# A causal attention block with top-2 expert layer: scores and row maxima of two heads in the two halves of the array's rows, the mask added by VectorE, and maxima three blocks ahead

## The chip, the cores and the metric

One core of a Trainium2 chip runs the whole program. The metric is the device time of one execution in microseconds; three executions of the kernel before gave 769.35, 771.28 and 776.9 us, median 771.28.

## What is computed

The input is x of 8 sequences x 512 rows x 128 columns, fp32. Attention has 16 heads of 8 dimensions with rotary embedding, a causal mask and softmax. Its result is added to x and layer-normalized. Then every row goes through a shared expert and through the two best of 8 routed experts (hidden width 256), and is layer-normalized again.

```python
q = rope(x @ Wq); k = rope(x @ Wk); v = x @ Wv      # 16 heads of 8
attn = softmax(where(causal, q @ k.T / 8 ** 0.5, -inf))
x = layernorm(x + (attn @ v) @ Wo)
rw, sel = top_k(x @ router_w.T + bias, 2); rw = softmax(rw)
ffn = lambda w1, w3, w2: (silu(x @ w1) * (x @ w3)) @ w2
x = layernorm(x + ffn(shared) + sum over r of rw[r] * ffn(expert sel[r]))
```

## The kernel before, in words

**Order of the work.** Nothing is scheduled at run time. The program lays events on a clock of its own, whose unit is one score unit (a full PSUM bank of 512 score columns, 40 to a sequence, 320 in all). The table `AT` gives each kind of event its place on that clock and `LATER` shifts a kind on one engine; each engine issues its events in that order (`line`), and semaphores do the rest. So an engine's instructions stand in a fixed row, and one that waits holds up all behind it.

**Attention.** q and k are projected with two fp32 matmuls each (L652), turned by VectorE (L877), summed and split into three bf16 parts that add up to the fp32 value (L315, L319, L323, with ScalarE's L542 and L546). SyncE stores the parts to a scratch in DRAM (L343) and loads them back (L356) as `stack`: for each head the six products of parts in `SLOTS`, 8 dimensions each, in 96 rows with zeros between (L1038, L1059, L448), and three more rows for the maxima. A half is 8 heads of a sequence; `stack` has three places for halves.

**Maxima.** For each head and each of four blocks of 128 queries the row maximum must be known before the exponential. `max_unit` fills one of two PSUM banks (`M`): first a matmul of the identity with the mask writes the upper triangle's -3e38 (L675), and the score matmuls of 96 rows are accumulated on top (L679). There are 22 units to a half, 352 in all. VectorE reduces each unit with one instruction (L884). When a half is through, its maxima are transposed (L686), split in three bf16 parts (L893 to L896) and written by DMA into rows 96 to 98 of `stack` (L362).

**Scores.** `scores_unit` computes the transposed scores less the maximum with 99 rows (L698) into one of two PSUM banks (`SC`), ScalarE takes the exponential (L529), GpSimd zeroes the triangle of the diagonal blocks (L465). After ten units, four heads are done and `weighted_values` multiplies them with v (L712, fp32, four heads in the four groups of 32 columns of the array).

**The rest.** Heads are transposed and normalized (L724, L908), projected (L738), added and normalized (L930, L914, L924). The expert layer goes in 131 steps of 128 rows: gate and up matmuls (L806), tanh (L586), products (L1008, L1013, L1016), down (L818), copy (L594, L599). Rows are scattered to the experts' places by indirect DMA (L477) and gathered back (L487), summed (L1025).

What sets the order around the change: in `AT`, the stack of the first half is loaded at -35.81 units (4.19 - 40) before its sequence's scores and its maxima start at -32.27; those of the second half at -20.48 and -14.26. Max units are laid evenly over their stretch of the clock, one by one, among score units.

## Time and profile before

| | us |
|---|---|
| median of the three runs shown | 771.28 |
| the profiled execution | 781.67 |
| its span, first to last instruction | 779.8 |
| TensorE (PE) matmuls busy | 618.9 |
| VectorE (DVE) busy | 478.6 |
| ScalarE (ACT) busy | 329.6 |
| GpSimd (POOL) busy | 333.2 |
| mean granted TensorE clock | 0.900 of full |

PE is matmuls, PEld the loads of its stationary operand, SPq the DMA issues of SyncE's queue. Busy time is not path: matmuls overlap each other, and the recorded length of one holds its passage through the array too, so the distance between the starts of two matmuls says more than their lengths. In the chain of work that ended last, each piece is followed back to what released it.

### The profile page before, as it was taken

The numbers are of one execution on the slowest core, as the hardware profiler recorded it, in microseconds if no ns is written. First come the engines' busy times: TensorE is split into PE (matmuls) and PEld (weight loads), VectorE is DVE, ScalarE is ACT, GpSimd is POOL, SyncE is SP. The second block draws the span as 40 slices with busy tenths as digits, with TensorE's granted clock in tenths as the row PEclk, the third lists the DMA queues.
The fourth block names the chain that finished last, engine by engine and source line by source line (L and its number), as shares of the span: only waits on it lengthen the run. The fifth ranks groups of instructions, "written<-read, shape, count | busy, mean of one in ns | idle before, by whom it ended". The sixth has DMA issues, their size and how long they took to land.

```text
span 779.8 us, 14442 instructions
## 1 busy us (share of the span) xinstructions
PE 618.9 (79%) x4715; PEld 431.3 (55%) x4715; DVE 478.6 (61%) x1290; ACT 329.6 (42%) x771; POOL 333.2 (43%) x531
## 2 busy tenths in 40 slices
PE   3397997996969899998796989896998877776750
PEld 1132445644626576676564766675677665575740
DVE  7476685784727577875476788673676631563352
ACT  2003663563326445753463445642564454322320
POOL 9013262262475222524676324327446443633304
PEclk9575998999979999999899999998998998979895
DMA  2642102102134535343345333523475355546641
GB/s 67 184 139 96 55 16 84 55 2 96 44 119 119 156 85 160 105 145 86 125 129 181 106 113 100 177 77 112 156 206 153 107 148 166 149 116 180 189 135 54
DMA packets 77256, 91.49 MB, mean 117 GB/s; under 512 B 9728, under 2 KB 60544, under 8 KB 75648
## 3 DMA queue, kind: packets, MB, share of 16 engines
q1 hardware_dynamic: 73088, 82.19, 35.8%
q0 software_dynamic: 4096, 8.40, 3.6%
q8 instruction: 38, 0.62, 0.3%
q14 instruction: 34, 0.28, 0.1%
HBM read 68.08 MB, written 22.09 MB: 116 GB/s over the span
## 4 chain that ended last, share of the span: by engine, by line
PE 44%; DVE 16%; issue 12%; POOL 11%; DMA 9%; SPq 4%; ACT 3%; another core or an unknown queue 2%; POOLq 0%; DVEq 0%; ACTq 0%
PE ps L806 10%; PE ps L818 6%; PE ps L712 6%; PE ps L679 5%; PE ps L698 5%; POOL yg L487 4%; DMA stack<-parts_scratch 4%; DMA parts_scratch<-parts 3%; PE ps L675 3%; PE ps L652 3%; SPq L356 3%; DVE negmax L884 3%; POOL rows_in L477 2%; POOL parts L323 2%
## 5 line engine op out<-in xcount | busy, mean ns | idle before, releaser
L884 DVE TENSOR_REDUCE negmax<-ps 128x1 f32<-128x384 f32 (+3 forms) x352 | 214.9, 638 | 104.2 <-PE ps L679 91.3
L465 POOL TENSOR_SCALAR_AFFINE_SELECT probs<-probs 128x256 f32<-128x256 f32 (+1 forms) x320 | 115.1, 365 | 280.1 <-ACT probs L529 277.2
L529 ACT ACTIVATE probs<-ps 128x512 f32<-128x512 f32 x320 | 186.7, 598 | 81.7 <-PE ps L698 75.4
L679 PE MATMUL ps<-stack 96*128 96x512 bf16 (+3 forms) x512 | 139.1, 328 | 0.0
L698 PE MATMUL ps<-stack 99*128 99x384 bf16 (+3 forms) x512 | 127.5, 314 | 6.2 <-issue 4.1
L675 PE MATMUL ps<-mask_bf,ident_bf 128*128 128x128 bf16 (+2 forms) x352 | 93.1, 265 | 45.5 <-issue 20.5
L806 PE MATMUL ps<-xgT,w_tile 128*128 128x128 f32 x792 | 114.6, 291 | 9.2 <-issue 5.9
L806 PEld LDWEIGHTS ps<-xgT,w_tile 128*128 128x128 f32 x792 | 106.6, 205 | 14.4 <-issue 7.3
L1008 DVE SCALAR_TENSOR_TENSOR gate<-th,ps 128x256 f32<-128x256 f32 x131 | 54.5, 416 | 95.7 <-ACT th L586 71.7
L586 ACT ACTIVATE th<-ps 128x256 f32<-128x256 f32 x131 | 50.2, 383 | 107.7 <-PE ps L806 97.2
L818 PE MATMUL ps<-w_tile,hid 128*128 128x128 f32 x396 | 68.8, 298 | 30.2 <-DVE hid L1016 24.2
L675 PEld LDWEIGHTS ps<-mask_bf,ident_bf 128*128 128x128 bf16 x352 | 35.7, 101 | 100.1 <-DVE negmax L884 40.5
L487 POOL DMA_INDIRECT yg<-rows_out,slot x64 | 61.4, 960 | 45.3 <-DVE acc L1025 16.6
L712 PE MATMUL ps<-probs,va 128*32 128x512 f32 (+3 forms) x1024 | 78.7, 449 | 2.4 <-POOL probs L465 2.1
L818 PEld LDWEIGHTS ps<-w_tile,hid 128*128 128x128 f32 x396 | 54.8, 199 | 44.2 <-DVE hid L1016 34.3
L477 POOL DMA_INDIRECT rows_in<-x,slot x64 | 62.9, 982 | 28.0 <-issue 14.2
L698 PEld LDWEIGHTS ps<-stack 99*128 99x128 bf16 x512 | 50.8, 103 | 21.5 <-issue 7.2
L679 PEld LDWEIGHTS ps<-stack 96*128 96x128 bf16 x512 | 51.2, 105 | 13.5 <-issue 3.6
L712 PEld LDWEIGHTS ps<-probs,va 128*32 128x32 f32 x1024 | 30.9, 112 | 48.8 <-issue 39.0
L599 ACT ACTIVATE y_routed<-ps 128x128 f32<-128x128 f32 x99 | 27.6, 279 | 58.1 <-PE ps L818 37.0
L559 ACT ACTIVATE ot<-ps 128x512 f32<-128x512 f32 x32 | 19.1, 597 | 67.9 <-PE ps L712 59.7
L1016 DVE TENSOR_TENSOR hid<-gate,ps 128x256 f32<-128x256 f32 x99 | 41.7, 421 | 3.4
(111 smaller groups left out, 721.1 us busy)
## 6 DMA issues: line engine op xcount, KB each, us to landing
w_tile<-in_experts SPq DMA_DIRECT2D x99, 384.0 KB
stack<-parts_scratch SPq DMA_DIRECT2D x96, 128.0 KB
rows_out<-y_routed SPq DMA_DIRECT2D x99, 64.0 KB
parts_scratch<-parts SPq DMA_DIRECT2D x8, 768.0 KB, 4.6
xg<-rows_in SPq DMA_DIRECT2D x21, 256.0 KB, 4.6
rows_in<-zeros SPq DMA_DIRECT2D x2, 1472.0 KB, 11.2
x_t<-in_x SPq DMA_DIRECT2D x8, 256.0 KB, 3.0
x_r<-in_x SPq DMA_DIRECT2D x8, 256.0 KB, 4.7
```

What stands on the lines that cost most here:

```text
L465: pool.affine_select(out=area, in_=area, compare_op=ALU.is_ge, fill=0.0, base=0, pattern=pattern, channel_multiplier=-1).then_inc(masked, 1)
L477: pool.indirect_dma_start(out=rows_in[g % 2], out_offset=bass.IndirectOffsetOnAxis(ap=slot[:, r, s, t:t + 1], axis=0), in_=x1[:, s % X1RIN ...
L487: pool.indirect_dma_start(out=yg[:, t, r, :], out_offset=None, in_=rows_out[g % 2], in_offset=bass.IndirectOffsetOnAxis(ap=slot[:, r, s, t ...
L529: act.activation(probs[:, (s * NB + v) % PRING, :], ps[:, SC + v % 2, :], ACT.Exp, scale=SCALE).then_inc(exp_done, 1)
L675: pe.matmul(diagonal, ident_bf[:, :], mask_bf[:, :].rearrange("p (o s) -> p o s", o=1).broadcast_to([P, n, P]), start=True, stop=False, sk ...
L679: last = pe.matmul(unit[:, at:at + w], stack[0:KZ, n_half % PLACES, 0, h0 + k - HH * (u // NAH), i * P:(i + 1) * P], stack[0:KZ, n_half % ...
L698: last = pe.matmul(unit[:, at:at + S - j * P], here[:, 1, j * P:(j + 1) * P], here[:, 0, j * P:S], start=True, stop=True)
L712: last = pe.matmul(ps[32 * k:32 * k + 32, bank("values", s, g), j * P:S], va[:, j, PER_PV * g + k, :], probs[:, (s * NB + v) % PRING, at:a ...
L806: last = pe.matmul(ps[:, GU + i % 2, j * P:(j + 1) * P], w[:, j * P:(j + 1) * P], moving, start=True, stop=True)
L818: last = pe.matmul(ps[:, bank("down", i), 0:D], hid[:, i % HRING, half * P:(half + 1) * P], w[:, (4 + half) * P:(5 + half) * P], start=(ha ...
L884: dve.tensor_reduce(negmax[:, h0:h0 + n, i], unit[:, :, 0:(i + 1) * P], AX_X, ALU.max, negate=True).then_inc(m_free, 1)
L1008: link(dve.scalar_tensor_tensor(out=gate[:, i % 2, :], in0=th[:, i % 2, :], scalar=1.0, in1=bank[:, 0:2 * P], op0=ALU.add, op1=ALU.mult), ...
```

## The change

- **Layout.** `stack` has 128 rows: rows 0 to 63 hold one head, rows 64 to 127 another, each with 8 dimensions x 8 slots (six products, a seventh slot for the maxima, an eighth of zeros). A place holds 4 such pairs. The seventh slot comes from a fixed part `flat` (zeros for q, ones for k), stored once to the scratch; it is loaded with the others, so a half is loaded by 7 DMAs of 16 x 2 x 2048 instead of 6 of 8 x 2 x 4096, and the parts are stored by 2 DMAs instead of 1. The maxima are written over the q side of that slot, two rows at a time. The weights' columns are permuted on the host to fit.
- **Bursts.** A block is four heads, ten units. `burst` issues two units one after the other, the first from rows 0 to 63, the second from rows 64 to 127, each into its own PSUM bank; five bursts of scores and five of maxima to a block.
- **Maxima.** The mask matmul is gone, and units are cut as those of scores are (320 units in place of 352). VectorE runs one `tensor_tensor_reduce` for each piece: it adds the mask (`mask_sb`, fp32 in SBUF), negates, takes the minimum, and writes the sum as bf16 to `sums`, which nobody reads. Each is built as two instructions, the pass itself and one with a 128x1 output: 512 + 512 in place of 352.
- **Lead.** Maxima run three blocks (30 units) ahead of their scores.
- **Order.** The table `AT` is a new one: the stack of the first half at -39.65 with its maxima from -29 on, that of the second at -15.2 with its maxima from -9 on; routed steps are laid by `spread`, and the last group's gathers have places of their own. Memsets of `stack` on VectorE (L1038, L1059) and the bf16 copies of identity and mask (L1051, L1052) are gone; GpSimd clears `stack` in three memsets.

```diff
-SLOTS = [(0, 0), (0, 1), (1, 0), (1, 1), (0, 2), (2, 0)]
+SLOTS = [(0, 0), (0, 1), (1, 0), (1, 1), (0, 2), (2, 0), (3, 3)]
...
+    MAX_UNITS = [[(0, 3, 0)], [(1, 3, 0)], [(0, 2, 0), (0, 0, 3 * P)], [(1, 2, 0), (1, 0, 3 * P)],
+                 [(0, 1, 0), (1, 1, 2 * P)]]
+    PAIR_UNITS = [[(0, 0, 0)], [(1, 0, 0)], [(0, 1, 0), (0, 3, 3 * P)], [(1, 1, 0), (1, 3, 3 * P)],
                   [(0, 2, 0), (1, 2, 2 * P)]]
+    BLOCKS = H // 4
+    LEAD = 3
...
+            add(now + v - v % 2 + 0.02 * (v % 2) - 2 * NU * LEAD + 1, "max", s, v)
...
+    for n in range(BLOCKS * B + LEAD):
+        for b in range(NU):
+            add(2 * (NU * (n - LEAD) + b), "burst", n, b, "scores")
+            add(2 * (NU * (n - LEAD) + b) + 1, "burst", n, b, "max")
...
-        stack = sb("stack", [KM, PLACES, 2, HH, S], BF16)
+        stack = sb("stack", [P, PLACES, 2, HH // 2, S], BF16)
...
-                pe.matmul(diagonal, ident_bf[:, :], mask_bf[:, :].rearrange("p (o s) -> p o s", o=1).broadcast_to([P, n, P]),
-                          start=True, stop=False, skip_group_check=True)
...
+            def score(bank, half, pair, slot, stationary, at_s, moving, at_m, width, at):
+                here = stack[KS * pair:KS * pair + KS, half % PLACES, :, slot, :]
+                return pe.matmul(ps[:, bank, at:at + width], here[:, stationary, at_s:at_s + P],
+                                 here[:, moving, at_m:at_m + width], start=True, stop=True)
+            def burst(n, b, part):
...
+                    for pair in range(2):
+                        if first + pair >= 2:
+                            pe.wait_ge(exp_done, first + pair - 1)
+                        for at_piece, (k, j, at) in enumerate(PAIR_UNITS[b]):
+                            last = score(SC + pair, half, pair, 2 * (block % 2) + k, 1, j * P, 0, j * P, S - j * P, at)
+                        last.then_inc(st_ps, 1)
...
+                    for pair in range(2):
+                        use = m_use[("max", s, 2 * NU * block + 2 * b + pair)]
+                        bank_free(use)
+                        for k, i, at in MAX_UNITS[b]:
+                            last = score(M + use % 2, half, pair, 2 * (block % 2) + k, 0, i * P, 1, 0, i * P + P, at)
+                        last.then_inc(m_full, 1)
...
-                dve.tensor_reduce(negmax[:, h0:h0 + n, i], unit[:, :, 0:(i + 1) * P], AX_X, ALU.max,
-                                  negate=True).then_inc(m_free, 1)
+                if use >= 2:
+                    dve.wait_ge(m_free, use - 1)
+                for k, i, at in MAX_UNITS[b]:
+                    h, w = HH * (block // 2) + HH // 2 * pair + 2 * (block % 2) + k, i * P + P
+                    ins = dve.tensor_tensor_reduce(sums[:, use % 2, at:at + w], ps[:, M + use % 2, at:at + w],
+                                                   mask_sb[:, S - w:S], -1.0, 3.0e38, ALU.add, ALU.min,
+                                                   negmax[:, h:h + 1, i])
+                ins.then_inc(m_free, 1)
```

PE in the middle of the program, before: max units (L675 with L679) and score units (L698) in turn, with steps of the expert layer (L789, L806, L818) between.

```order
L698 MATMUL ps<-stack 128x384 [waits exp_done]
L698 MATMUL ps<-stack 128x128
L675 MATMUL ps<-mask_bf,ident_bf 128x128 [waits m_free]
L679 MATMUL ps<-stack 128x384
L698 MATMUL ps<-stack 128x512 [waits exp_done]
L675 MATMUL ps<-mask_bf,ident_bf 128x128 [waits m_free]
L679 MATMUL ps<-stack 128x384
L789 MATMUL ps<-ident_sb,xg 128x128 [waits ring_free1,rows_here0]
L818 MATMUL ps<-w_tile,hid 128x128 [waits ring_free0,hid_done]
```

PE after, at a like place; L687 is `score`, and a wait on exp_done marks a score unit, one on m_free a max unit.

```order
L687 MATMUL ps<-stack 128x256 [waits exp_done]
L687 MATMUL ps<-stack 128x256
L687 MATMUL ps<-stack 128x256 [waits exp_done]
L687 MATMUL ps<-stack 128x256
L839 MATMUL ps<-w_tile,hid 128x128 [waits ring_free1,hid_done]
L839 MATMUL ps<-w_tile,hid 128x128
L810 MATMUL ps<-ident_sb,xg 128x128 [waits ring_free0,rows_here2]
L687 MATMUL ps<-stack 128x256 [waits m_free]
L687 MATMUL ps<-stack 128x256
L687 MATMUL ps<-stack 128x256 [waits m_free]
L687 MATMUL ps<-stack 128x256
```

Score and max units now come two by two, each pair with its two waits, the mask's matmul is gone, and other work stands between pairs and no longer between single units.

VectorE in the middle of the program, before: reduces (L884) between the products of expert steps.

```order
L1008 SCALAR_TENSOR_TENSOR gate<-th,ps 128x256 [waits th_done]
L1016 TENSOR_TENSOR hid<-gate,ps 128x256 [waits ring_full0,gate_done]
L884 TENSOR_REDUCE negmax<-ps 128x1 [waits m_full] x2
L1008 SCALAR_TENSOR_TENSOR gate<-th,ps 128x256 [waits th_done]
L1013 SCALAR_TENSOR_TENSOR hid<-gate,ps 128x256 [waits ring_full1,gate_done]
L884 TENSOR_REDUCE negmax<-ps 128x1 [waits m_full] x3
```

VectorE after, at a like place.

```order
L1030 SCALAR_TENSOR_TENSOR gate<-th,ps 128x256 [waits th_done]
L1038 TENSOR_TENSOR hid<-gate,ps 128x256 [waits ring_full0,gate_done]
L904 ISA sums,negmax<-ps,mask_sb 128x384 [waits m_free,m_full]
L904 ISA negmax 128x1
L904 ISA sums,negmax<-ps,mask_sb 128x128
L904 ISA negmax 128x1
L904 ISA sums,negmax<-ps,mask_sb 128x384 [waits m_free,m_full]
L904 ISA negmax 128x1
L904 ISA sums,negmax<-ps,mask_sb 128x128
L904 ISA negmax 128x1
L904 ISA sums,negmax<-ps,mask_sb 128x256 [waits m_free,m_full]
L904 ISA negmax 128x1
```

Each piece is a pass and a 128x1 instruction, a unit of two pieces is four instructions, and the products of an expert step (L1030, L1038) stand behind as many as 16 of them.

## Rows read from the trace of the kernel before

**Rows 1.** Busy time, share of the span and instructions.
```profile
PE 618.9 (79%) x4715; PEld 431.3 (55%) x4715; DVE 478.6 (61%) x1290; ACT 329.6 (42%) x771; POOL 333.2 (43%) x531
```

**Rows 2.** Busy time by stretch: PE, PEld, DVE, ACT, POOL, then clock.
```profile
0.00:67.00 67.00, 37.16 (x128) 13.15 (x129) 45.95 (x60) 6.91 (x8) 24.98 (x17) 0.70 0.41 126
67.00:666.00 599.00, 517.33 (x4122) 360.54 (x4120) 380.41 (x1033) 296.86 (x675) 267.29 (x469) 0.94 0.38 113
666.00:780.00 114.00, 64.45 (x468) 57.64 (x468) 52.25 (x199) 25.83 (x89) 40.90 (x46) 0.83 0.47 134
...
400.00:500.00 100.00, 86.61 (x726) 61.09 (x725) 74.07 (x199) 52.18 (x122) 48.27 (x79) 0.98 0.47 135
```

**Rows 3.** The chain that ended last, by engine and by line.
```profile
PE 44%; DVE 16%; issue 12%; POOL 11%; DMA 9%; SPq 4%; ACT 3%; another core or an unknown queue 2%; POOLq 0%; DVEq 0%; ACTq 0%
PE ps L806 10%; PE ps L818 6%; PE ps L712 6%; PE ps L679 5%; PE ps L698 5%; POOL yg L487 4%; DMA stack<-parts_scratch 4%; DMA parts_scratch<-parts 3%; PE ps L675 3%; PE ps L652 3%; SPq L356 3%; DVE negmax L884 3%; POOL rows_in L477 2%; POOL parts L323 2%
```

**Rows 4.** Costliest groups: out<-in xcount | busy, mean ns | idle before, releaser.
```profile
L884 DVE TENSOR_REDUCE negmax<-ps 128x1 f32<-128x384 f32 (+3 forms) x352 | 214.9, 638 | 104.2 <-PE ps L679 91.3
...
L679 PE MATMUL ps<-stack 96*128 96x512 bf16 (+3 forms) x512 | 139.1, 328 | 0.0
L698 PE MATMUL ps<-stack 99*128 99x384 bf16 (+3 forms) x512 | 127.5, 314 | 6.2 <-issue 4.1
L675 PE MATMUL ps<-mask_bf,ident_bf 128*128 128x128 bf16 (+2 forms) x352 | 93.1, 265 | 45.5 <-issue 20.5
```

**Rows 5.** PE and the DMA of the stack: total wait, times, longest.
```profile
PE ps L675 <- DMA stack<-parts_scratch: 15.1, 7, 4.5
```

**Rows 6.** One such wait in order of time: SPq's issues, PE, ScalarE.
```profile
180.26 4.28 SPq L356 DMA_DIRECT2D stack<-parts_scratch  x6
...
187.63 0.61 PE L675 MATMUL ps<-mask_bf,ident_bf 128*128 128x512 bf16 x1 [4.50 <-DMA stack<-parts_scratch]
...
189.13 0.60 ACT L529 ACTIVATE probs<-ps 128x512 f32<-128x512 f32 x1 [5.36 <-PE ps L698]
```

**Rows 7.** PE in order of time from 300.7 us: start, length, instruction.
```profile
300.89 2.36 PE L712 MATMUL ps<-probs,va 128*32 128x512 f32 x32
303.19 0.23 PE L675 MATMUL ps<-mask_bf,ident_bf 128*128 128x128 bf16 x1
303.25 0.38 PE L679 MATMUL ps<-stack 96*128 96x512 bf16 x1
303.47 0.38 PE L698 MATMUL ps<-stack 99*128 99x512 bf16 x1
```

**Rows 8.** VectorE groups by form, with their means in ns.
```profile
L884 DVE TENSOR_REDUCE negmax<-ps 128x1 f32<-128x512 f32 x128 | 83.8, 687 | 41.9 <-PE ps L679 35.6 <-remote 3.0 <-issue 1.7
L884 DVE TENSOR_REDUCE negmax<-ps 128x1 f32<-128x384 f32 x128 | 67.7, 551 | 19.4 <-PE ps L679 15.7 <-remote 2.1 <-issue 0.8
L1008 DVE SCALAR_TENSOR_TENSOR gate<-th,ps 128x256 f32<-128x256 f32 x131 | 54.5, 416 | 95.7 <-ACT th L586 71.7 <-issue 23.8
L1025 DVE SCALAR_TENSOR_TENSOR acc<-yg,rw,acc 128x128 f32<-128x128 f32 x64 | 18.3, 349 | 16.2 <-DMA yg<-rows_out,slot 16.0
L908 DVE TENSOR_TENSOR on<-ps,rden 128x128 f32<-128x128 f32 x32 | 7.8, 286 | 0.5
L960 DVE FIND_INDEX8 topi<-top,logits 128x8 uint32<-128x8 f32 x32 | 4.5, 162 | 0.0
L960 DVE MATCH_VALUE_LOAD topi<-top,logits 128x8 f32 x32 | 2.5, 78 | 0.3
```

**Rows 9.** The opening, in order of time: VectorE, ScalarE's first exponential.
```profile
32.60 0.69 DVE L884 TENSOR_REDUCE negmax<-ps 128x4 f32<-128x512 f32 x1 [8.50 <-PE ps L679]
...
41.84 6.56 DVE L884 TENSOR_REDUCE negmax<-ps 128x1 f32<-128x384 f32 x9 [0.24 <-PE ps L679]
...
67.22 0.60 ACT L529 ACTIVATE probs<-ps 128x512 f32<-128x512 f32 x1 [5.62 <-PE ps L698]
```

**Rows 10.** VectorE busy with L884 alone, from 67 to 666 us.
```profile
67.00:666.00 599.00, 190.95 (x313) 0.94 0.38 113
```

More of the change, by code:

```diff
@@ new lines @@
+LATER = {("act", "T"): 0.17, ("act", "ln1"): -0.2, ("act", "ln2"): -0.31, ("act", "out"): -0.33, ("act", "rest"): 2.75,
+         ("act", "rope"): 2.16, ("act", "weights"): 0.16, ("act", "x_T"): -0.18, ("dve", "count"): -0.5,
+         ("dve", "max_rows"): -0.5, ("dve", "rank"): 0.28, ("dve", "router"): -0.5, ("pool", "ln2"): -0.33,
+         ("pool", "low"): -0.29, ("pool", "product"): 1.64, ("pool", "rest"): 0.55, ("pool", "rope"): -0.5,
+         ("pool", "scores"): 0.76, ("pool", "shared_rows"): 0.44}
@@ L441, in _ @@
         def _(pool):
+            pool.memset(flat[:, 0, :].bitcast(F32), 0.0).then_inc(flat_set, 1)
+            pool.memset(flat[:, 1, :].bitcast(F32), TWO_ONES).then_inc(flat_set, 1)
             pool.memset(minus_half[:, :], -0.5).then_inc(setup_p, 1)
+            for n in range(PLACES):
+                pool.memset(stack[:, n, :, :, :].bitcast(F32), 0.0).then_inc(stack_p, 1)
             pool.memset(va[:, :, :, :], 0.0).then_inc(setup_p, 1)
@@ new lines, in score @@
+            def score(bank, half, pair, slot, stationary, at_s, moving, at_m, width, at):
[3 more added lines that the diff above has]
+            def burst(n, b, part):
+                scored = n - LEAD
+                if part == "scores" and scored >= 0:
+                    s, block = scored // BLOCKS, scored % BLOCKS
+                    half = scored // 2
+                    first = NU * 2 * scored + 2 * b
+                    if scored % 2 == 0 and b == 0:
+                        pe.wait_ge(max_in, (half + 1) * 48)
+                    for pair in range(2):
[4 more added lines that the diff above has]
+                        last.then_inc(st_ps, 1)
+                if part == "max" and n < BLOCKS * B:
+                    s, block = n // BLOCKS, n % BLOCKS
+                    half = n // 2
+                    if n % 2 == 0 and b == 0:
+                        pe.wait_ge(stacked[half % PLACES], STACK * (half // PLACES + 1))
+                    for pair in range(2):
+                        use = m_use[("max", s, 2 * NU * block + 2 * b + pair)]
[3 more added lines that the diff above has]
+                        last.then_inc(m_full, 1)
@@ L823, in _ @@
             for kind, key in line("pe"):
-                if kind == "max":
-                    max_unit(*key)
+                if kind == "burst":
+                    burst(*key)
                 elif kind == "max_rows":
                     max_rows(*key)
-                elif kind == "scores":
-                    scores_unit(*key)
                 elif kind == "values":
```

201 lines of the change are left out of this document (82 added, 119 removed).

## The prediction

> **What bounds the kernel now.** I read the busy table first [rows 1]: PE is busy 79% of the span, VectorE 61%, ScalarE 42%, GpSimd 43%. The busy time by stretch [rows 2] splits the span at the first and the last exponential: 67 us of opening, 599 us of main part, 114 us of end. In the main part PE is busy 517 of 599 us (86%) and VectorE 380 (64%). The busiest 100 us that I found for VectorE, 400 to 500, has it at 74%, with PE at 87%: no stretch has VectorE as its bound. The chain that ended last [rows 3] agrees: 44% PE, 16% VectorE, 12% "issue", 9% DMA. On it the mask matmul L675 has 3%, the max matmul L679 5%, the score matmul L698 5%, the reduce L884 3%. So PE is the bound, with VectorE behind it, and the change takes work from the first and gives some to the second.
>
> **The sum is made against the profiled execution,** 781.67 us, of which 779.8 are span; the median of the runs shown is 771.28, so a result is multiplied by 771.28 / 781.67 = 0.987. A measurement of this kernel can tell about 1% (8 us) from no change.
>
> **1. The mask matmuls go.** There are 352, 93.1 us of records [rows 4], but records overlap. By starts, one 128 wide takes 303.25 - 303.19 = 0.06 us, and a matmul 512 wide takes 303.47 - 303.25 = 0.22 us [rows 7]. With 256 masks of 128 columns, 64 of 256 and 32 of 512 that is 15 + 7 + 7 = 29 us of PE. The chain gives them 3% of 779.8 us, 23 us [rows 3]. I take 26, the middle of 23 and 29, which are the bounds.
>
> **2. Two heads side by side.** A half had 5120 columns of scores for each four heads, and as many for the maxima, all one behind the other. If matmuls on rows 0 to 63 and on 64 to 127 run together but start in order, a burst of one piece each (512 and 512) takes 512 columns in place of 1024; a burst of 384 + 128 twice takes 768, because the second head's first piece waits until the first head's last one starts; one of 256 + 256 takes 512 to 768. Two, two and one of them make 3072 to 3328 in place of 5120: 35 to 40% less. L679 and L698 have 5% each of the chain [rows 3], together 78 us, and 37% of that is 28 us. The bounds are 0 (no overlap at all) and 31. For overlap speaks a row: the 32 matmuls of L712, on four groups of 32 columns, take 303.19 - 300.89 = 2.3 us [rows 7]. Each of the 16 products has on average 320 columns and is built as two fp32 instructions, each of which runs over the columns at least once; at 0.22 us for 512 columns, 32 x 320 columns would already take 4.4 us one behind the other. The array does work on several column groups together here; row groups are not in this trace.
>
> The Trainium skill (TensorEngine Tiling, Key Properties) says that changing the tiling mode drains the engine. Every burst stands between 128-row matmuls. In this trace PE goes from 32-column tiles to the full array at 303.19 with no gap before the mask matmul [rows 7], so for that form the drain doesn't show; for 64 rows no run here shows it.
>
> **3. The stall at the head of a half.** Seven times PE waited for the stack's DMA, 15.1 us in all, up to 4.5 us each [rows 5]. In one of them six loads are issued from 180.26 on, and the first max unit starts at 187.63 [rows 6]: 7.4 us. Before, the clock leaves 3.5 units (-35.81 to -32.27) between them, 6.6 us at 599 / 320 = 1.87 us a unit, which is too little. The new table leaves 10.65 units (19.9 us) for the first half and 6.2 (11.6 us) for the second; a seventh load adds one issue, 4.28 / 6 = 0.71 us, so 8.1 us are needed. The 15.1 us go, and with them some slow matmuls after each stall (0.61 us for the mask at 187.63), say 3 us: 18. Bounds 0 (something else is late: the store, which is two DMAs now, or the projections) and 20. What is late next is VectorE, the next part.
>
> **4. VectorE.** The new pass is not in the trace. Its operands (PSUM and SBUF, both fp32) are those of L1008, 416 ns for 256 columns, and L908, 286 for 128; the reduce took 687 for 512 and 551 for 384 [rows 8]. The slope, (687 - 286) / 384 = 1.04 ns a column, holds throughout. One head is 687 + 551 + 416 + 286 = 1940 ns, 128 heads 248 us. Then the 512 instructions with a 128x1 output. The nearest rows are 78 ns (MATCH_VALUE_LOAD, the small companion of another instruction) and 162 (FIND_INDEX8) [rows 8]; I take 100, nearer to the companion, so 51 us, bounds 40 and 83. Together 299 us in place of 214.9 [rows 4]: VectorE gains 84 us, between 73 and 116. How much of it reaches the path? Today 16% of the span over 478.6 us busy, 26%, of VectorE's time is on the chain [rows 1, 3]; if the path went through it like its share of the span it would be 61%. I take the middle, 43%: +36 us, bounds 19 (73 at 26%) and 71 (116 at 61%). Behind a pass that waits stand the products of an expert step, and PE's down matmul waits for these.
>
> The Trainium skill (Vector Engine (DVE) Microarchitecture Reference, the pitfalls at its end) says that an instruction of this struct shape with two non-bf16 sources in SBUF runs at half rate. L1025 has two and takes 349 ns for 128 columns where L908 takes 286; L1008, with one of its two in PSUM, stays on the slope. By this the new pass would keep full rate.
>
> **5. What costs nothing.** The memsets and casts that leave VectorE lie in the opening before the first reduce at 32.60 [rows 9], where the stack's DMA ends last. Then three blocks of maxima, 12 heads, must pass before the first exponential: 12 x (1.94 + 0.4) = 28 us and about 5 us for the rope products and the splitting, so 32 + 33 = 65 against 67.2 [rows 9]. The larger mask load and the store of `flat` lie beside the projection. The end, 114 us [rows 2], has no maxima and hardly changes. GpSimd and ScalarE keep their work, at 45 and 50% of the main part [rows 2].
>
> **The sum:** 781.7 - 26 - 28 - 18 + 36 = 745.7 us, times 0.987 = **736 us**. A check on VectorE: in the main part it has 380.4 us, of which 191 are reduces [rows 2, 10]; 116 heads remain there, 116 x 2.34 = 271, so 461 us. The main part would be 599 - 36 = 563, with VectorE at 82%. That is more than the 74% seen anywhere, and is the weak point. What speaks for it is the opening: there 9 reduces stand in 6.56 us without a gap [rows 9], even with PE at half clock, and bursts bring two banks at a time.
>
> **The rivals.**
> - *VectorE becomes the bound (slower).* The max banks are two, and a burst needs both. PE stands at the second bank's wait until VectorE is through with the last burst, then its other work is late, and VectorE in turn waits for the gates. If VectorE reaches no more than the 74% of its busiest stretch [rows 2], the main part is 461 / 0.74 = 623 us, and with 65 and 112 us around it 800, plus 2 outside the span, x 0.987 = 791 us, 2.6% slower. It decides from where VectorE's reachable share falls under 461 / 599 = 77%. For it: the two shares in 400 to 500 us, 87 and 74%, have never been nearer than that. Against it: PE was what ended there.
> - *VectorE hides more.* Additional cost 19, pairs 31, masks 29, stall 20: 781.7 - 61 = 720.7, and some 5 us of PE's waits at banks go as the lead is longer: 716 x 0.987 = 706 us.
> - *The halves don't run together.* Part 2 is worth nothing, and each of some 320 bursts costs one more small gap of 0.06 us (the smallest distance in rows 7), 19 us at PE's share of the chain, 44%: +8. That gives 781.7 - 26 - 18 + 36 + 8 = 782, x 0.987 = 772 us: no change. For it: no row of this trace has two row groups. Against it: L712.
> - *The pass runs at half rate.* Then 163,840 columns cost 1.04 ns more each, 171 us. VectorE's main part is 461 + 155 = 616 us; at 85% that is 725, in all 904 x 0.987 = 892 us. Against it: L1008.
>
> **How the numbers follow.** My forecast (faster, 715 to 755) 0.43; VectorE hides more 0.21; the halves don't run together 0.10; VectorE as the bound 0.20; half rate 0.03; the stall stays or moves, with the rest as forecast (about 752 us) 0.03. Faster by over 1% comes from the first two and the last, 0.67; within 1% is 0.10; slower by over 1% 0.23. The range runs from 692, a little under the second case, to 791, the fourth; half rate and an upper tail of the fourth are left out.
>
> **What would show it.** Right: L675 gone; starts of the two matmuls of a one-piece burst under 0.1 us apart (0.22 if they don't run together); no wait of PE for the stack's DMA; the pass near 690 ns at 512 columns with its companion near 100 (wrong for half rate: 1.2 us); VectorE's busy time near 550 us and above 80% of the main part; its waits for the max matmuls, 91.3 us now [rows 4], under 50. Wrong: PE's waits for VectorE's pass grow above 50 us and VectorE stays near 75%; first exponential far from 65 us.

## The result and the profile after

The kernel after took 808.75 us, median of 4 executions (808.29 to 810.16); the kernel before, run beside it, 773.93. The ratio is 1.046, with a 95% interval of 1.041 to 1.052. It is slower, where 736 us were forecast, and it lies above the range of 692 to 791. Chips differ: the same kernel before took between 761 and 783 us on them. So what follows compares either runs made on one chip, or ratios to the kernel before on the same chip. An execution falls in one of two states, a faster and a slower one; ratios and granted clocks below are of the faster, medians are of all.

First the page of the kernel after: busy time, then the chain by engine and by line.

```profile
PE 631.3 (78%) x4363; PEld 392.2 (49%) x4363; DVE 474.8 (59%) x1957; ACT 326.5 (41%) x771; POOL 321.2 (40%) x530
...
PEclk8556887989987979998996789998799999968995
...
PE 51%; DVE 19%; issue 16%; POOL 5%; ACT 4%; another core or an unknown queue 2%; DMA 2%; SPq 1%; POOLq 0%; DVEq 0%; ACTq 0%
PE ps L827 13%; PE ps L733 11%; PE ps L687 8%; DVE sums L904 6%; PE ps L839 6%; PE ps L674 5%; POOL yg L507 2%; DVE gate L1030 2%; PE ps L745 2%; ACT th L608 1%; PE ps L774 1%; POOL rows_in L497 1%; DVE acc L1047 1%; DVE negmax L904 1%
```

TensorE has 352 matmuls fewer than before [rows 1] and is yet busy for 12 us more; its share of the chain rose from 44 to 51% [rows 3]. VectorE did not get the 550 us that I expected: 474.8, less than before. The lines that grew on the chain are not those of the change (L687 has 8%, where L679, L698 and L675 had 13%) but the expert layer's gate and up matmuls (L827 after, L806 before: 10 to 13%) and the product with v (L733, before L712: 6 to 11%). Nothing was edited in them.

The same stretches as in [rows 2], cut at the first and the last exponential of this kernel:

```profile
0.00:61.00 61.00, 32.00 (x75) 9.61 (x75) 30.26 (x106) 6.91 (x8) 14.76 (x16) 0.65 0.49 145
61.00:691.00 630.00, 531.76 (x3823) 321.81 (x3820) 391.72 (x1654) 293.41 (x675) 265.66 (x470) 0.88 0.37 111
691.00:806.00 115.00, 67.59 (x468) 60.79 (x468) 52.82 (x199) 26.22 (x89) 40.77 (x45) 0.81 0.46 134
```

The opening is 6 us shorter, the end 1 us longer, and the main part has 630 us in place of 599. All of the loss is there. Its granted clock fell from 0.94 to 0.88. The clock has two levels in the records, 1.2 and 2.4 GHz, so a mean of 0.850 over 806 us is 2 x 0.15 x 806 = 242 us at the lower one; before it was 2 x 0.10 x 780 = 156.

Costliest groups after (compare [rows 4]), and the waits of TensorE and VectorE (engine and line, released by, total, times, longest):

```profile
L904 DVE CUSTOM_DVE_ANT_0 sums<-ps,mask_sb 128x384 bf16<-128x384 f32 (+3 forms) x512 | 221.7, 486 | 87.4 <-PE ps L687 75.4
L687 PE MATMUL ps<-stack 64*128 64x512 bf16 (+3 forms) x1024 | 171.0, 335 | 55.0 <-DMA stack<-parts_scratch 17.3
L733 PE MATMUL ps<-probs,va 128*32 128x512 f32 (+3 forms) x1024 | 92.1, 507 | 11.3 <-POOL probs L485 4.4
L904 DVE DVE_READ_ACCUMULATOR2_ANT negmax<- 128x1 f32 x512 | 42.3, 83 | 0.0
```

```profile
PE ps L687 <- DMA stack<-parts_scratch: 17.3, 1, 17.3
PE ps L687 <- DVE negmax L904: 11.6, 39, 1.1
PEld ps L687 <- DVE negmax L904: 40.5, 81, 1.6
PEld ps L687 <- ACT probs L549: 25.5, 47, 3.5
DVE gate L1030 <- ACT th L608: 102.9, 73, 5.0
DVE sums L904 <- PE ps L687: 75.4, 40, 11.3
```

The seven stalls for the stack [rows 5] are gone; the one of 17.3 us left is the opening's. VectorE waits 75 us for scores and 103 for ScalarE's tanh (before 71.7 [rows 8]): it is far from being the bound. The weight loads of the score and max matmuls wait 40.5 us for its maxima, which is what they waited before:

```profile
PEld ps L675 <- DVE negmax L884: 40.5, 92, 2.3
```

And its pass with its companion, in order of time:

```profile
30.21 0.69 DVE L904 CUSTOM_DVE_ANT_0 sums<-ps,mask_sb 128x512 bf16<-128x512 f32 x1 [11.34 <-PE ps L687]
30.83 0.08 DVE L904 DVE_READ_ACCUMULATOR2_ANT negmax<- 128x1 f32 x1
30.83 0.69 DVE L904 CUSTOM_DVE_ANT_0 sums<-ps,mask_sb 128x512 bf16<-128x512 f32 x1
31.44 0.08 DVE L904 DVE_READ_ACCUMULATOR2_ANT negmax<- 128x1 f32 x1
31.61 0.69 DVE L904 CUSTOM_DVE_ANT_0 sums<-ps,mask_sb 128x512 bf16<-128x512 f32 x1
```

The 512-wide pass takes 0.69 us, as forecast, but the companion of 0.08 starts together with the next pass, 0.61 to 0.62 us after the first. The pair costs 0.62, not 0.79. A record is longer than the distance to the next start for plain reduces too: in the kernel before two of 512 columns, each 0.69 long, start 0.60 to 0.61 us apart where nothing holds the second back.

Last, TensorE at a burst, its matmuls and then its weight loads:

```profile
302.82 0.61 PE L827 MATMUL ps<-x1T,w_shared 128*128 128x128 f32 x4
303.36 0.39 PE L687 MATMUL ps<-stack 64*128 64x512 bf16 x2
303.68 0.33 PE L810 MATMUL ps<-ident_sb,xg 128*128 128x128 f32 x1
```

```profile
303.35 0.10 PEld L687 LDWEIGHTS ps<-stack 64*128 64x128 bf16 x2
303.68 0.14 PEld L810 LDWEIGHTS ps<-ident_sb,xg 128*128 128x128 f32 x1 [0.23 <-issue]
```

The halves do run together: two matmuls of 512 columns in 0.39 us. But the next full matmul starts 0.32 us after them, where it would start after 0.22 in the full array [rows 7], and its weights are loaded only then, at 303.68, and not during the matmul before. In the kernel before, the load for the full-array matmul at 303.47 [rows 7] starts at 303.25, 0.22 us ahead of it.

### The profile page after: what moved, and what is told of

It is laid out like the page before. It is cut to its first block, busy times and chain, and to the rows that moved or that the text cites. A ratio compares the mean times of both kernels' runs of the same rounds, so it can differ in the third digit from the quotient of the medians.

```text
span 806.3 us, 14746 instructions
## 1 busy us (share of the span) xinstructions
PE 631.3 (78%) x4363; PEld 392.2 (49%) x4363; DVE 474.8 (59%) x1957; ACT 326.5 (41%) x771; POOL 321.2 (40%) x530
## 3 DMA queue, kind: packets, MB, share of 16 engines
q0 software_dynamic: 4096, 8.40, 3.4%
## 4 chain that ended last, share of the span: by engine, by line
PE 51%; DVE 19%; issue 16%; POOL 5%; ACT 4%; another core or an unknown queue 2%; DMA 2%; SPq 1%; POOLq 0%; DVEq 0%; ACTq 0%
PE ps L827 13%; PE ps L733 11%; PE ps L687 8%; DVE sums L904 6%; PE ps L839 6%; PE ps L674 5%; POOL yg L507 2%; DVE gate L1030 2%; PE ps L745 2%; ACT th L608 1%; PE ps L774 1%; POOL rows_in L497 1%; DVE acc L1047 1%; DVE negmax L904 1%
## 5 line engine op out<-in xcount | busy, mean ns | idle before, releaser
L904 DVE CUSTOM_DVE_ANT_0 sums<-ps,mask_sb 128x384 bf16<-128x384 f32 (+3 forms) x512 | 221.7, 486 | 87.4 <-PE ps L687 75.4
L687 PE MATMUL ps<-stack 64*128 64x512 bf16 (+3 forms) x1024 | 171.0, 335 | 55.0 <-DMA stack<-parts_scratch 17.3
L827 PE MATMUL ps<-xgT,w_tile 128*128 128x128 f32 x792 | 124.2, 306 | 8.9 <-issue 6.2
L1030 DVE SCALAR_TENSOR_TENSOR gate<-th,ps 128x256 f32<-128x256 f32 x131 | 54.7, 417 | 122.2 <-ACT th L608 102.9
L827 PEld LDWEIGHTS ps<-xgT,w_tile 128*128 128x128 f32 x792 | 109.2, 213 | 22.4 <-issue 18.2
L687 PEld LDWEIGHTS ps<-stack 64*128 64x128 bf16 x1024 | 47.6, 96 | 147.6 <-DVE negmax L904 40.5
L733 PE MATMUL ps<-probs,va 128*32 128x512 f32 (+3 forms) x1024 | 92.1, 507 | 11.3 <-POOL probs L485 4.4
L733 PEld LDWEIGHTS ps<-probs,va 128*32 128x32 f32 x1024 | 35.0, 123 | 68.6 <-issue 55.3
L827 PE MATMUL ps<-x1T,w_shared 128*128 128x128 f32 x256 | 43.9, 326 | 0.0
L1038 DVE TENSOR_TENSOR hid<-gate,ps 128x256 f32<-128x256 f32 x99 | 41.6, 420 | 3.4
L904 DVE DVE_READ_ACCUMULATOR2_ANT negmax<- 128x1 f32 x512 | 42.3, 83 | 0.0
L894 DVE TENSOR_TENSOR qk<-ps,cos_sb 128x512 f32<-128x512 f32 x16 | 11.1, 692 | 52.4 <-PE ps L674 42.0
L827 PEld LDWEIGHTS ps<-x1T,w_shared 128*128 128x128 f32 x256 | 39.1, 233 | 4.3 <-issue 3.2
```

Source lines behind the costliest of these rows:

```text
L687: return pe.matmul(ps[:, bank, at:at + width], here[:, stationary, at_s:at_s + P], here[:, moving, at_m:at_m + width], start=True, stop=True)
L733: last = pe.matmul(ps[32 * k:32 * k + 32, bank("values", s, g), j * P:S], va[:, j, PER_PV * g + k, :], probs[:, (s * NB + v) % PRING, at:a ...
L827: last = pe.matmul(ps[:, GU + i % 2, j * P:(j + 1) * P], w[:, j * P:(j + 1) * P], moving, start=True, stop=True)
L904: ins = dve.tensor_tensor_reduce(sums[:, use % 2, at:at + w], ps[:, M + use % 2, at:at + w], mask_sb[:, S - w:S], -1.0, 3.0e38, ALU.add, A ...
L1030: link(dve.scalar_tensor_tensor(out=gate[:, i % 2, :], in0=th[:, i % 2, :], scalar=1.0, in1=bank[:, 0:2 * P], op0=ALU.add, op1=ALU.mult), ...
L1038: dve.tensor_tensor(hid[:, i % HRING, :], gate[:, i % 2, :], bank[:, 2 * P:4 * P], ALU.mult).then_inc(hid_done, 1)
```

## The experiments

Three theories went into them. **S**: every change of the tile's form on TensorE (from 64 rows to the full array or back) costs a fixed time, about 0.1 us. The trace of before has 90 changes of form, all from its 32-column tiles, that of after 479 (some expectations use a first count, 84 and 473; the difference is the same 389). **C**: TensorE with less work in the array is granted the lower clock for longer, and that is the loss. **O**: the order, bursts of two units with the waits between them, sets the time.

### The rows as the only difference

`a1_full_rows` issues every score and max matmul over all 128 rows, and is otherwise the kernel after.

```diff
-                here = stack[KS * pair:KS * pair + KS, half % PLACES, :, slot, :]
+                here = stack[0:P, half % PLACES, :, slot, :]
```

> The changed kernel, but each score and max matmul reads all 128 rows of the stack instead of 64, so that the two heads of a pair can't run side by side and the array never changes to 64-row tiles (each product then sums two heads: the part left out is the separation of the heads; the instructions, their order and their number stay). Theory S (changes of tile form cost about 0.1 us each, some 390 more than before): 37 us of drains go, some 50 us of streaming come back, so 5 to 15 us slower than the changed kernel, with the same clock. Theory C (the array is filled less, so the clock falls; half-speed time rose by 87 us): the clock rises from 0.85 to 0.90 or more and the time falls by 15 to 40 us. Theory O (the order in bursts of two with its waits on ScalarE and VectorE sets the time, whatever PE does): within 5 us of the changed kernel.

Measured: 785.76 beside 780.86, ratio 1.006 (1.002 to 1.010), against after's 1.046. The changes of form are 90 again, and most of the loss is gone. It was theory C whose forecast came true here: 15 to 40 us faster than after with the clock near 0.90 (0.899 in the middle, where after has 0.844). Theory S had it slower than after. On another chip it was run again beside the kernel after itself and beside `a7_one_half`, in which both heads are taken from rows 0 to 63 (`stack[0:KS, ...]`), so that the changes of form stay and the overlap goes.

> The changed kernel once more, on the same chip as the next three, so that their differences are read on one chip. All theories: 1.04 to 1.05 of the kernel before.

> The changed kernel with all score and max matmuls on 128 rows (heads summed), once more beside it: 1.003 to 1.01 of the kernel before, as in the first run.

> The changed kernel with both heads of a pair read from rows 0 to 63 (the second head's result is the first's: that part is left out), so that every change between full and 64-row form stays and no two matmuls can overlap. Against a1_again it has the changes alone, against the changed kernel it lacks the overlap alone. Theory S (changes cost, overlap gains): slower than the changed kernel by 10 to 35 us, since some 50 us of streaming come back. Theory C (the overlap empties the array and the clock falls): within 8 us of the changed kernel, with less half-speed time; the overlap then brings nothing.

On one chip, with before at 781.17: a1 786.01 (1.007), after 810.96 (1.040), a7 837.98 (1.071). So 64-row tiles without overlap cost 837.98 - 786.01 = 52 us, the overlap gives back 837.98 - 810.96 = 27, and 25 are left. The 27 are at nearly one clock (0.840 and 0.845), but the 52 hold two things: 389 changes of form, and a clock of 0.840 in place of 0.897. This time theory S's forecast came true (10 to 35 us slower than after) and theory C's (within 8) did not. In a7 a pair takes 1.03 us at the lower clock and the work behind it starts 0.96 us after it:

```profile
300.77 1.03 PE L687 MATMUL ps<-stack 64*128 64x512 bf16 x2
301.73 2.07 PE L827 MATMUL ps<-x1T,w_shared 128*128 128x128 f32 x8
```

The main parts of a1_again and a7_one_half, in the columns of [rows 2]:

```profile
61.00:667.00 606.00, 500.27 (x3772) 338.72 (x3820) 390.38 (x1651) 289.47 (x674) 266.32 (x470) 0.94 0.39 115
```

```profile
61.00:719.00 658.00, 588.39 (x3806) 347.57 (x3804) 392.48 (x1651) 293.66 (x671) 264.57 (x466) 0.86 0.36 105
```

VectorE, ScalarE and GpSimd have the same busy time in both to within 5 us; TensorE alone gains 88 us (a little less in truth: 48 matmuls of a1_again left no record here, x3772 against x3820 weight loads).

### What one change of form costs

`m1_tiles` is the kernel before with test matmuls in its opening, where TensorE otherwise waits (12 to 31 us), in several patterns.

```diff
+                for n in range(8):
+                    tile(0, 0, 64, 0, P, S)
+                    tile(1, 64, P, 0, P, S)
+                for n in range(6):
+                    tile(4, 0, P, 0, P, P)
+                    tile(0, 0, 64, 0, P, S)
+                    tile(1, 64, P, 0, P, S)
```

> The kernel before, with some 120 test matmuls on PE in the idle stretch between the first projections and the first maxima (13 to 31 us): after a run of full ones, rows of a 128-column full matmul followed by two of 512 columns, the two either on all 128 rows, on 96 rows, or one on rows 0 to 63 and one on 64 to 127, and by four 32-column ones. Theory S: a pair on row halves starts within 10 ns of each other, but every change between full and 64-row form costs 0.09 to 0.1 us, so full, half, half takes as long as full, full, full within 0.05 us; 96 rows cost no change. Theory C expects besides that the first maxima, which follow at once, run at full clock, and the first exponential comes 2 to 6 us earlier than 67.2; the whole kernel is then faster by 2 to 6 us. Theories S and O: no change of the whole.

Six full matmuls of 512 columns and twelve of 64 rows, each a piece of its own:

```profile
14.28 1.46 PE L826 MATMUL ps<-test 128*128 128x512 bf16 x6
...
16.97 1.47 PE L826 MATMUL ps<-test 64*128 64x512 bf16 x12
```

Within a run of pairs the halves are worth a full factor of two. Between full matmuls they are not. Times from one start to the next in ns, from the records of this run:

```
full 128, full 512, full 512          55  216  216   period 0.488 us
full 128, lo 512,   hi 512           162    3  319   period 0.484 us
full 128, 96-row 512, 96-row 512      58  219  215   period 0.492 us
full 128, four 32-column 512     159  3  3  3  322   period 0.49 us
```

Each change costs 162 - 55 = 107 or 319 - 216 = 103 ns, for 32-column tiles as for 64 rows; 96 rows cost nothing. A pair of 512 between full matmuls, the best burst of the change, thus gains 216 ns by the overlap and loses 210 by its two changes: next to nothing. Only two of the five bursts of a block are of this kind. A burst of 384 + 128 twice saves 256 columns, half as much, and so, by the same numbers, loses 0.1 us.

The kernel after shows the price too. At the higher clock a 64-row matmul starts 207 ns after a full one of 128 fp32 columns, where the next full one starts after 112, and a full one 317 ns after a 64-row one of 512 columns, where it is 216 behind a full one: 95 and 101 ns. At the lower clock it is 353 against 213 and 536 against 427 (the last from a1_again): 140 and 109. So the lower clock doesn't double the price of a change, while it does double that of the columns.

The test run took 1.001 of before (0.998 to 1.005), and its first exponential stood at 66.90, though its granted clock was 0.924 where before had 0.911 on that chip: a TensorE kept at the higher clock in the opening brings nothing.

`a6_form_changes` puts one 64-row matmul of 16 columns ahead of each score burst of a1; its result is overwritten.

> a1_full_rows (all matmuls on 128 rows, heads summed) with one small matmul of 64 rows and 16 columns ahead of each burst of scores, into a bank that is then overwritten: 320 changes of tile form more and next to no work. Theory S: 0.095 us each, 30 us of PE, so 15 to 30 us slower than a1_full_rows, back near the changed kernel, with the clock nearly as in a1. Theory C: within 8 us of a1_full_rows, since the array's streaming work is the same.

Measured 1.025 (1.018 to 1.031) beside a1's 1.006 on another chip: about 1.9%, 14 us (8 to 21 by the intervals), for 160 added matmuls and 313 added changes. That is 0.09 us for each insertion with its two changes, 0.045 a change, less than the 0.21 and 0.105 of the test. A part is hidden in a wait that was there anyway: the weight loads of scores and maxima wait 8.9 us for the exponential, where they wait 21.6 in a1_again. The granted clock was 0.909 to 0.914, that of before on the same chip 0.907 to 0.919: the changes alone don't lower it. Theory S's forecast (15 to 30 us) is missed by 1 us and lies within the interval, theory C's 8 us only at its edge.

### The clock

`a2_max_twice` issues the max matmuls of each burst twice (`for _ in range(2)`), over the same banks.

> The changed kernel, but the matmuls of each max unit are issued twice in a row into the same bank (the second overwrites the first with the same values). About 160 bursts get 0.2 to 0.3 us more PE work, 30 to 45 us in all, with no further change of tile form. Theory S: slower by 20 to 45 us. Theory C: the clock rises (0.87 or more) and the time changes by less than 10 us, or falls. Theory O: PE's own work has slack, so slower by under 10 us with the clock unchanged or higher.

Measured 1.035 (1.028 to 1.043), no slower than after's 1.040 and 1.046, although some 35 us of array time were added (160 bursts at 0.22 us). The granted clock was 0.885 to 0.892, where after has 0.842 to 0.853. The forecasts of theories C and O came true, S's 20 to 45 us did not. With a7 at 0.834 to 0.841 and a1 at 0.891 to 0.904 this fits theory C as an amplifier, though a6, whose changes came with the full array at work, kept the clock of before: a kernel that leaves more of the array unused seems to get the higher clock for less of its time. But C alone would have let a7, whose array has the same work one behind the other, be as fast as after; it is 27 us slower.

How much is the clock's? The records of the clock, laid over those of TensorE's matmuls, give the busy time at each level. The last column counts the lower level's half, as work at 2.4 GHz; it is an estimate, and for the three kernels with 64-row tiles some 4 us too low, since a change of form doesn't double at the lower clock.

```
              busy us   at the lower clock   counted at the higher
before         618.9         103.3                567
after          631.3         190.4                536
after_again    634.9         199.2                535
a7_one_half    691.0         229.3                576
```

By this count the change took 31 us of work from TensorE, changes of form included; it is busy for 12 us more because 87 us more of its busy time lie at the lower clock. So even with the changes' price in it TensorE's work fell; what grew is the time that it takes over that work. How much of that reaches the kernel's time, and whether the clock fell because of the tiles or because TensorE waits more, no run here separates.

### The mask and VectorE's pass

`b1_dve_mask` is the kernel before with its own units, in which the mask matmul is gone and VectorE runs the new pass.

```diff
-                pe.matmul(diagonal, ident_bf[:, :], mask_bf[:, :].rearrange("p (o s) -> p o s", o=1).broadcast_to([P, n, P]),
-                          start=True, stop=False, skip_group_check=True)
...
-                dve.tensor_reduce(negmax[:, h0:h0 + n, i], unit[:, :, 0:(i + 1) * P], AX_X, ALU.max,
+                    ins = dve.tensor_tensor_reduce(sums[:, use % 2, at:at + w], ps[:, M + use % 2, at:at + w],
+                                                   mask_f[:, S - w:S], -1.0, 3.0e38, ALU.add, ALU.min,
```

> The kernel before with one part of the change alone: no mask matmul, VectorE adds the mask in a pass of its own for each head (512 passes and 512 reads in place of 352 reduces); order, layout and units as before. PE loses 29 us of streaming, VectorE gains about 7 us of busy time by the changed kernel's trace. Theories S and O: faster than before by 10 to 25 us, since PE was the bound. Theory C: the clock falls below 0.90 and the time is within 8 us of before or slower.

`b3_mask_kept` is b1 with the mask matmul still issued and overwritten.

> As b1_dve_mask (VectorE adds the mask in its pass), but PE still issues the mask matmul ahead of each max unit, now overwritten by the scores and so without effect: PE has 29 us more than in b1. Theory C: the clock is back at 0.90, and the time is that of b1 or shorter by up to 8 us. Theories S and O: slower than b1 by 5 to 20 us, since PE does more and VectorE the same.

b1 took 1.009 (1.005 to 1.012), b3 1.014 (1.006 to 1.022). The exchange costs 0.85%, 7 us. The 352 mask matmuls are worth 0.6%, 4 to 5 us of the 29 that they take (b1 and b3 ran on two chips, and within the intervals it may be zero), and the pass costs b3's 1.4%, 11 us. Most of the masks' time is thus not missed when it goes.

The clock says where a part of it went. Without the mask matmuls b1 was granted 0.885, where before had 0.902 on that chip; with them b3 had 0.911, as before had on its own. Of b1's 783 us that is 2 x 0.017 x 783 = 27 us more at the lower clock. Theory C forecast this for both runs; S and O had forecast b1 faster than before by 10 to 25 us.

### The stall

`b2_early_stack` is the kernel before with the store of the parts and the stack of the first half issued earlier.

```diff
-          low=-2.87, store_parts=3.09, stack0=4.19, max0=7.73, ...
+          low=-2.87, store_parts=0.3, stack0=0.4, max0=7.73, ...
```

> The kernel before with two numbers of its table changed: the store of the parts 2.79 units and the load of the first half's stack 3.79 units earlier. My sum gave 18 us for the stall at the head of a half; if that term holds by itself, faster by 8 to 18 us. If the load was late because its data were late (the projections and GpSimd's sums ahead of it), under 5 us.

Measured 0.998 (0.994 to 1.002). But it didn't do what I meant:

```profile
PE ps L675 <- DMA stack<-parts_scratch: 12.6, 6, 4.7
```

The stall is 12.6 us in six waits where it was 15.1 in seven [rows 5], so this run says little of what its end is worth. Its time fits the expectation's second case (under 5 us), that the load was late because its data were. The runs with the new table say more, at the end of this section.

### The order of the bursts

`a3_adjacent` is the kernel after with the burst of maxima directly behind the burst of scores, `a5_adjacent_full` the same over 128 rows (a1's edit).

```diff
-            add(2 * (NU * (n - LEAD) + b) + 1, "burst", n, b, "max")
+            add(2 * (NU * (n - LEAD) + b) + 0.001, "burst", n, b, "max")
```

> The changed kernel, but each burst of maxima stands directly behind its burst of scores on every engine's clock (0.001 in place of 1 unit later), so that about half of the changes of tile form go (some 200 of 470). Theory S: faster by 12 to 20 us. Theory C: the array has longer empty stretches, clock the same or lower, time within 5 us or slower. Theory O: the gates of expert steps no longer stand between scores and maxima, PE waits more for VectorE's pass and for ScalarE: slower by 5 us or more.

> a3_adjacent (each burst of maxima directly behind its burst of scores) with all matmuls on 128 rows (heads summed). a3_adjacent was some 4.5% faster than the changed kernel. Theory S: that gain came from fewer changes of form, so without row halves the adjacent order brings nothing: within 8 us of a1_again. If the order itself gains (theory O): faster than a1_again by 10 us or more.

a3 took 0.999 (0.993 to 1.006): four units in one piece of TensorE's row make the kernel after as fast as before. It has 325 changes of form in place of 479. a5 took 771.64 beside a1_again's 786.01, 14.4 us less, where the number of changes is the same (90): this part is the order alone. From after to a3 it is 4.1 to 4.7% (1.040 and 1.046 to 0.999), 32 to 36 us; the 18 to 22 more go with 154 fewer changes, 0.12 to 0.14 us each, and with a clock of 0.864 in place of 0.845. Theory S had forecast 12 to 20 us in all and O a loss; O's forecast for a5 (10 us or more) came true.

Is there a kernel in this that beats before? `c1_full_adjacent` computes everything, with the layout of before (96 and 99 rows, six slots), VectorE's pass, the new table and adjacent bursts. `c2_full_adjacent_pe_mask` is c1 with the mask added by TensorE and one plain reduce for each piece.

> The kernel after with the layout of the kernel before (one head at a time in 96 rows, 99 for scores, six slots, loads of 4096 elements) and with the burst of maxima laid directly behind the burst of scores, so that one piece of PE's row holds four units. The whole computation is done. If what a5 gained (1.3% under before) is due to the order alone and not to what it left wrong in the data, this gives 0.985 to 0.993 of before (theory O). If the gain was due to 128 rows in place of 96, or if the stack's loads in the layout of before bring back their stall, it gives 1.0 or more. PE should have no row tiles, some 84 changes of form as before (the 32-column ones), and a clock near 0.90.

> The same as c1_full_adjacent, but the mask is added by TensorE (320 mask matmuls of one or two diagonals) and VectorE reduces each piece with one plain reduce and no 128x1 instruction. From b1 and b3 the mask matmuls are worth 0.6% and VectorE's pass costs 1.4% in the layout of before, so this should be about 0.8% faster than c1: 0.977 to 0.987 of before. If PE is the bound and its instructions count in full, it is 20 us or more slower than c1 instead.

c1: 766.92 beside 761.92, 1.006 (1.002 to 1.010). c2: 773.99, 1.016 (1.010 to 1.021). Both expectations failed. c1 is not faster than before, and with adjacent bursts the mask on VectorE is better by 7 us, where in the order of before it was worse by 7. The clock moved with the masks here too (c2 0.919, c1 0.905), but didn't outweigh them. c1 was run again beside a5, and beside `c3_full_apart`, c1 with the maxima one unit behind (`+ 1` again), all on one chip.

> c1_full_adjacent once more, on the chip of the next two. If its 1.0056 belongs to the kernel, it stays within 0.5% of that (1.00 to 1.01); if chips differ in what they make of this order, it moves towards a5's 0.987.

> a5_adjacent_full once more (128 rows with both heads summed, so scores of the wrong sums; seven slots, loads of 2048). If the layout of before costs c1 something (loads, clears in the opening, 96 rows), this stays near 0.987 and so 1 to 2% under c1_again on this same chip. If the difference was the chip's, the two are equal.

> c1 with the burst of maxima one unit behind the scores, as the kernel after has it; the whole computation is done. From a1 against a5 the adjacent order gains 1.9% (some 15 us). If that holds whatever the layout, this is 1.5 to 2% slower than c1_again. If the order matters only with the layout of after, the two are equal.

Before 782.88; c1 777.24 (1.000, 0.992 to 1.008), a5 771.88 (0.980, 0.973 to 0.988), c3 790.05 (1.007, 1.004 to 1.011). The adjacent order is worth 12.8 us by the medians in the layout of before too, as it was 14.4 in that of after; the ratios give 6 us, and their intervals just allow both. No kernel that does the whole computation came out clearly under before; a5, which did, sums two heads. It is about 5 us faster than c1 in medians, half of it in the opening (first exponential at 58.24 and 60.66), and the intervals of the two ratios just miss each other; where the rest comes from stays open.

c3 has no stall for the stack outside the opening, 18.5 of these 19.4 us:

```profile
PE ps L684 <- DMA stack<-parts_scratch: 19.4, 2, 18.5
```

and yet its ratio (1.007) is that of b1 (1.009), which has the stalls, the order of before and the same pass. So stalls, bursts, lead and table together brought nothing that these runs can tell; what the end of the stalls is worth by itself was not measured.

## Why the prediction was wrong

**Part 2 is the step that failed.** I took the gain of side-by-side matmuls for 28 us (37% of 78 is 29), and it was 27 (a7 against after). That it came so near is partly luck: it was a share of the chain, not a count of columns at a clock. What I priced at nothing was the change of form, "for that form the drain doesn't show", and nowhere did the sum have a lower clock. Together these cost 52 us, the difference between a7 and a1_again, with 479 - 90 = 389 more changes and a clock of 0.840 in place of 0.897. At the test's 0.105 us the changes take 41 us of TensorE; at a6's 0.045, which is what reached the time there, 18. So by estimate 18 to 41 of the 52 are the changes, and the other 11 to 34 come with the lower clock; the split stays open.

I had looked at [rows 7] for a gap before the mask matmul at 303.19, but a row merges 32 matmuls and its length covers the last one's passage; between the start of the last 32-column matmul and that of the next full one the records of before have 202 to 205 ns, where full matmuls of that kind follow in 112. The price of a change stood in the trace of before, one level below the row that I read. The rule that I had set against it, of the Trainium skill (TensorEngine Tiling, Key Properties), that changing the tiling mode drains the engine, was right: the test has 0.10 us for each change of form, and none between tiles of one form (3 ns).

**Parts 1 and 4 were both too large, and nearly right in sum.** Masks: 26 forecast, 4 to 5 measured (b3 against b1). The chain's 3% for L675 was time on the chain; when it went, the clock went down with it (b1). The pass: 36 forecast, 11 measured. Together +10 was forecast and +7 measured (b1): that the two errors cancel is luck. VectorE's busy time was mis-sized by 75 us (550 forecast, 474.8 measured). The companion, 51 us in the sum, runs beside the next pass, and the passes, 248 us by the lengths of records, are busy for 221.7, since records overlap: 0.62 us for both at 512 columns from start to start, as much as the plain reduce's 0.60 to 0.61. The full rate of the pass was forecast rightly; two fp32 sources in SBUF were not tried, and L1025's 349 ns against 286 [rows 8] are 63 ns more, where half rate would be 133 more (an estimate: 128 columns at 1.04 ns).

**Part 3, the stall: the waits went, their worth is not shown.** The seven waits went, as forecast, but no 18 us came of it: c3, without them, is as slow as b1, with them. Either their end is worth nothing, or the bursts, the lead and the table cost as much as it gave. TensorE also waits elsewhere: in after its score matmuls' weight loads wait 25.5 us for the exponential, where that was 6.0 before:

```profile
PEld ps L698 <- ACT probs L529: 6.0, 12, 1.9
```

**Part 5** was near: first exponential forecast at 65, found at 61.1; end of 114 us forecast unchanged, found at 115.

The sum as measured, against before's 781: exchange of mask and pass +7, stall with bursts, lead and table about -2 (a1's +5 less 7), 64-row tiles with their changes of form and lower clock +52, overlap -27, in all +30: 811. That it meets after_again's 810.96 proves nothing, since the terms are differences of neighbouring runs and must add up. The forecast had -36 in their place.

**The rivals.** VectorE as the bound had the right sign and came nearest to the time (791; its own terms, with an end of 114 us and not 112, give 793) for a wrong reason: VectorE is at 59%, waits 75 us for scores, and is waited for no longer than before. "The halves don't run together" had half of the reason, the cost of a burst among full matmuls, but at 0.06 us a burst on 44% of the path, some 8 us, where it was 18 to 41, and it denied the overlap, which is there. No rival combined overlap with a price for each change; that one would have been worth two short lines of arithmetic, 389 x 0.1 - 28 = +11, and the sign of part 2 would have turned. No rival had the clock fall when TensorE's work goes.

## What to carry to other kernels

Row tiles pay only in long runs: count the changes of form on TensorE, at 0.1 us each, against the columns saved between two of them; a lone pair of 512 columns among full matmuls just breaks even. Don't carry the granted clock over unchanged from the kernel before: here it went from 0.902 to 0.885 when the mask matmuls alone were taken out, and to 0.844 with the whole change. Read such prices from starts of single matmuls, never from a row that merges many. Where an engine is busy 86% but waits for others in between, its removed instructions are worth a fraction of their time (here 4 to 5 of 29 us); where its units stand (adjacent or apart) was worth 13 us with no instruction changed.

## What the runs showed of the hardware that I had not expected

- Row tiles on two banks start 3 to 4 ns apart (m1); a change from or to them costs 103 to 107 ns at 2.4 GHz there and 95 to 101 in the kernel after, the same as for 32-column tiles; 96 rows are not a change. At 1.2 GHz a change costs 109 to 140 ns.
- The weights of the next full matmul are not loaded during a 64-row matmul (load and matmul both start at 303.68; between full matmuls the load is 0.22 us ahead).
- VectorE's accumulator read (83 ns) runs beside the next pass, so a pass that adds the mask and reduces, followed by its read, costs 0.61 to 0.62 us at 512 columns, as much as a plain reduce from start to start (0.60 to 0.61).
- Removing work from TensorE lowered its clock: 0.902 to 0.885 without the mask matmuls (b1), 0.911 as before with them (b3); 0.844 after, and 0.887 when the max matmuls were issued twice (a2), which cost no time. What exactly the clock responds to was not tried.
